# Eighteen chunks of neighbour rows fetched one row at a time instead of fifteen, with part of the issuing moved to ScalarE

## What is computed

```python
def gnn(x, edge_index, ...):
    src, dst = edge_index
    agg = segment_sum(x[src], dst, num_segments=6250)
    h = relu(agg @ W_rel + b_rel + x @ W_root)
    i, f, g, o = split(h @ W_ih.T + b_ih + b_hh, 4)
    c = sigmoid(i) * tanh(g)
    return (sigmoid(o) * tanh(c)) @ W_fc + b_fc
x = x + gnn(layernorm(x), stack([src, dst]), ...)
x = x + slice_attention(layernorm(x), ...)
```

## Time and profile before

| | us |
|---|---|
| Runs before | 1247.07, 1250.91, 1253.03 |
| Median | 1250.91 |
| The profiled execution | 1246.6 |
| Its span, first to last instruction | 1244.8 |
| Around the span | 1.8 |

### The profile page before, as it was taken

The page is one execution under the profiler, slowest core; times in us unless marked ns, Lnnn a source line. Parts: engine busy times, 40 slices in busy tenths (PEclk is TensorE's granted clock), DMA queues, the critical chain, the costliest instruction groups (busy, mean ns, idle before and its releaser), DMA issues. The chain is left out here.

```text
span 1244.8 us, 30252 instructions
## 1 busy us (share of the span) xinstructions
PE 1113.5 (89%) x9821; PEld 970.4 (78%) x9821; DVE 833.0 (67%) x2580; ACT 627.7 (50%) x1257; POOL 793.0 (64%) x836
## 2 busy tenths in 40 slices
PE   1056889999999999999999999999999999999998
PEld 0045778788888887888888877888888888897798
DVE  7885466677566856776667666766676667646665
ACT  6862435545454545544554455445645554545332
POOL 5367777777777777777777777777777777400000
PEclk9997899999999999999999999999999999999999
DMA  9574444544554445444544454444444554223498
GB/s 329 205 248 120 123 117 147 150 133 122 150 150 140 128 139 148 139 128 136 150 142 138 126 150 139 141 126 148 140 140 127 148 147 137 90 60 99 129 347 291
DMA packets 92942, 188.74 MB, mean 152 GB/s; under 512 B 20890, under 2 KB 55567, under 8 KB 92797
## 3 DMA queue, kind: packets, MB, share of 16 engines
q0 software_dynamic: 39168, 107.01, 30.4%
q1 hardware_dynamic: 42770, 59.89, 14.8%
q10 hardware_dynamic: 10859, 20.05, 4.5%
HBM read 154.87 MB, written 32.00 MB: 150 GB/s over the span
## 5 line engine op out<-in xcount | busy, mean ns | idle before, releaser
L676 POOL DMA_INDIRECT ring<-table,sidx x798 | 765.3, 959 | 266.0 <-issue 260.3
L414 PE MATMUL ps<-h_h,wih_h 128*128 128x250 f32 x1200 | 338.2, 282 | 0.0
L415 PE MATMUL ps<-h_l,wih_h 128*128 128x250 f32 x1200 | 336.0, 280 | 0.0
L416 PE MATMUL ps<-h_h,wih_l 128*128 128x250 f32 x1200 | 336.0, 280 | 0.0
L414 PEld LDWEIGHTS ps<-h_h,wih_h 128*128 128x128 f32 x1200 | 229.6, 191 | 2.0 <-issue 0.8
L415 PEld LDWEIGHTS ps<-h_l,wih_h 128*128 128x128 f32 x1200 | 229.6, 191 | 1.1
L416 PEld LDWEIGHTS ps<-h_h,wih_l 128*128 128x128 f32 x1200 | 229.5, 191 | 0.0
L820 ACT ACTIVATE gate<-ps,bgate 128x250 f32<-128x250 f32 x300 | 124.4, 468 | 138.3 <-PE ps L416 138.3
L1048 PE MATMUL ps<-ring,oneh 128*32 128x512 f16 x2280 | 147.3, 386 | 46.3 <-DMA ring<-table,sidx 35.5
L1475 DVE TENSOR_SCALAR oneh<-iota,didx 128x64 f16<-128x64 f16 (+2 forms) x1199 | 183.5, 259 | 0.9 <-issue 0.9
L1048 PEld LDWEIGHTS ps<-ring,oneh 128*32 128x32 f16 x2280 | 61.3, 97 | 114.4 <-DMA ring<-table,sidx 48.0
(11 more groups left out here) (212 smaller groups left out, 2499.2 us busy)
## 6 DMA issues: line engine op xcount, KB each, us to landing
sp_ring<-table SPq DMA_DIRECT2D x1920, 1.0 KB
ring<-table,sidx POOLq DMA_INDIRECT x798
swt_d<-swt ACTq DMA_DIRECT2D x25, 500.0 KB
gate<-swt_d SPq DMA_DIRECT2D x19, 500.0 KB, 5.7
x_room<-in_x SPq DMA_DIRECT2D x12, 512.0 KB, 10.5
xn<-table SPq DMA_DIRECT2D x25, 224.0 KB
xin<-in_x SPq DMA_DIRECT2D x25, 224.0 KB
res<-xin SPq DMA_DIRECT2D x25, 224.0 KB
```

The costliest lines, as they stand in the source:

```text
L414: eng.matmul(dst, wh, xh, start=first, stop=False)
L415: eng.matmul(dst, wh, xl, start=False, stop=False)
L416: return eng.matmul(dst, wl, xh, start=False, stop=last)
L676: pool.indirect_dma_start(ring[:, j, :], None, table, bass.IndirectOffsetOnAxis(ap=idx, axis=0)).then_inc(done, 16)
```

## The change

SP_STEP goes from 52 to 42 and SP_N from 15 to 18, so chunks 86, 128, ..., 800 leave POOL's list: three more than before. Of each such chunk SP fetches 104 rows, in register loads of 26, and ACT the other 24: 12 rows in turn 0, then 20 rows a turn in three places (6 after `split_x`, 8 after gates 0 to 3 and `tanh_c` 0, 6 after gates 8 and 9), with one register load of 24 words at the start of each chunk. SP's places and numbers of rows in a turn stay. `wait_slot`, the wait for a free slot of `sp_ring`, is now done by both engines. ACT's loop over turns is written out. PE's waits for `sp_ring` still count all 128 rows.

```diff
-    SP_FIRST, SP_STEP, SP_N, SP_SLOTS = 86, 52, 15, 3
+    SP_FIRST, SP_STEP, SP_N, SP_SLOTS = 86, 42, 18, 3
...
-    ROWS_FIRST, ROWS, LOADS = 96, (8, 16, 60), 32
+    ROWS_FIRST, ROWS, LOADS = 96, (8, 16, 60), 26
+    SP_ROWS = 4 * LOADS
+    ACT_ROWS = P - SP_ROWS
+    ACT_FIRST, ACT_PARTS = 12, (6, 8, 6)
...
+        def wait_slot(eng, k):
+            if k == 0:
+                eng.wait_ge(spi_done, 1)
+            if k >= SP_SLOTS:
+                b = last_reader(SP_CHUNKS[k - SP_SLOTS])
+                eng.wait_ge(sum_done[b % 2], b // 2 + 1)
+                eng.wait_ge(sum_done[(b - 1) % 2], (b - 1) // 2 + 1)
+
+        def load_starts(eng, starts, k, q, n):
+            _, at = nc.values_load_multi_w_load_instructions(
+                sp_idx[k:k + 1, q:q + n], engines=[eng.engine], min_val=0, max_val=(N - 1) * row_bytes,
+                skip_runtime_bounds_check_because="the DMA checks its bounds")
+            starts[:] = at
+
+        def fetch_row(eng, k, q, start):
+            to = sp_ring[q:q + 1, k % SP_SLOTS, :].bitcast(U8)
+            eng.dma_start(to, rows8[ds(start, row_bytes)].rearrange("(p c) -> p c", p=1)).then_inc(
+                sp_rows[k % SP_SLOTS], 16)
...
             def fetch_rows(n):
 
-                for r in range(row_at[0], min(row_at[0] + n, SP_N * P)):
-                    k, q = r // P, r % P
+                for r in range(row_at[0], min(row_at[0] + n, SP_N * SP_ROWS)):
+                    k, q = r // SP_ROWS, r % SP_ROWS
...
+            row_at, starts = [0], [0] * ACT_ROWS
+
+            def fetch_rows(n):
+
+                for r in range(row_at[0], min(row_at[0] + n, SP_N * ACT_ROWS)):
+                    k, q = r // ACT_ROWS, r % ACT_ROWS
+                    if q == 0:
+                        wait_slot(act, k)
+                        load_starts(act, starts, k, SP_ROWS, ACT_ROWS)
+                    fetch_row(act, k, SP_ROWS + q, starts[q])
+                row_at[0] += n
+
             def turn(t, odd, gather, gnn, ffn, ahead):
...
+                if t == 0:
+                    fetch_rows(ACT_FIRST)
                 if gnn:
                     split_x(t - 1)
+                    fetch_rows(ACT_PARTS[0])
                     relu_h(t - 1, 0)
...
                     gates(t - 1, 0, 4)
                     tanh_c(t - 1, 0)
+                    fetch_rows(ACT_PARTS[1])
...
                     gates(t - 1, 8, 10)
+                    fetch_rows(ACT_PARTS[2])
...
-            with act.Fori(lo, hi, step) as t:
+            for t in range(lo, hi, step):
                 two_turns(turn, t)
```

More of the change, by code:

```diff
@@ L429, in store_chunk @@
                 eng.dma_start(table[RP * P:N, :], lt[TILES][0:REST, 0, :]).then_inc(ln_out[k % TILES], 16)
+        rows8 = table.bitcast(U8).rearrange("n c -> (n c)")
+        row_bytes = 4 * C
+        def wait_slot(eng, k):
[14 more added lines that the diff above has]
+                sp_rows[k % SP_SLOTS], 16)
         @block.sync
@@ L508, in _ @@
             row_at = [0]
-            rows8 = table.bitcast(U8).rearrange("n c -> (n c)")
-            row_bytes = 4 * C
             def fetch_rows(n):
-                for r in range(row_at[0], min(row_at[0] + n, SP_N * P)):
-                    k, q = r // P, r % P
+                for r in range(row_at[0], min(row_at[0] + n, SP_N * SP_ROWS)):
+                    k, q = r // SP_ROWS, r % SP_ROWS
                     if q == 0:
[L517 to L522, removed]
-                    if q % LOADS == 0:
[L524 to L530, removed]
+                        wait_slot(sp, k)
+                    if q % LOADS == 0:
+                        load_starts(sp, starts, k, q, LOADS)
+                    fetch_row(sp, k, q, starts[q % LOADS])
                 row_at[0] += n
@@ L539, in turn @@
                     for j, k in SP_OF.items():
-                        assert first_reader(j) // 2 > t or row_at[0] >= (k + 1) * P, (t, j, k, row_at)
+                        assert first_reader(j) // 2 > t or row_at[0] >= (k + 1) * SP_ROWS, (t, j, k, row_at)
                 if gather:
@@ L570, in _ @@
             last_turns(turn)
-            assert row_at[0] >= SP_N * P
+            assert row_at[0] >= SP_N * SP_ROWS
             def f_load(n, k):
@@ L843, in copy_out @@
                                ACT.Copy).then_inc(att_a, 1)
-            def turn(t, odd, gather, gnn, ffn, ahead):
+            row_at, starts = [0], [0] * ACT_ROWS
[7 more added lines that the diff above has]
+                row_at[0] += n
+            def turn(t, odd, gather, gnn, ffn, ahead):
+                if gather and t < NP - 1:
+                    for j, k in SP_OF.items():
+                        assert first_reader(j) // 2 > t or row_at[0] >= (k + 1) * ACT_ROWS, (t, j, k, row_at)
+                if t == 0:
+                    fetch_rows(ACT_FIRST)
                 if gnn:
                     split_x(t - 1)
+                    fetch_rows(ACT_PARTS[0])
                     relu_h(t - 1, 0)
@@ L906, in _ @@
             lo, hi, step = turns(turn)
-            with act.Fori(lo, hi, step) as t:
+            for t in range(lo, hi, step):
                 two_turns(turn, t)
             last_turns(turn)
+            assert row_at[0] >= SP_N * ACT_ROWS
             def f_high(n, k):
```

## The result

| us | before | after |
|---|---|---|
| Median | 1251.97 | 1296.74 |
| Lowest to highest of four runs | 1247.07 to 1253.08 | 1293.56 to 1299.77 |
| The profiled execution | 1246.6 | 1299.77 |
| Its span | 1244.8 | 1298.0 |

The ratio is 1.0364 [1.0334, 1.0394]: slower by 3.6%. The forecast was 1247.2 with a range up to 1255, so it is wrong, in sign and in size. Lines have moved: L1048 is now L1081, L676 is L688, L524 is L446, L529 is L453, L546, L556 and L564 are L558, L568 and L576, L1063 is L1096, L1125 is L1158, L829 is L841, L1066 is L1099, L778 is L790.

The account below looks back on a forecast made before the run. POOL's gather stream up to block 48, plus a fixed 181.45 us of PE's work, was taken to set the end. -3.75 us from POOL and 0 from the rest gave 1250.91 - 3.75 = 1247.2 us, range 1241.5 to 1255.

Parts of the forecast that it names:

- SP: SP's queue: 84 rows a turn, loads of 26 words at 1.81 us, 5.9 us a turn after 5.6, all covered.
- The cover: SP's wait for the next transposes, 108.5 us over 22 turns, 4.9 each, was to hide 0.3 us more of loads.
- The gathers that go: POOL's list: three gathers less up to PE's last wait, at block 48, 3.75 us saved; bounds 0 to 7.5 us.
- ACT's rows: ACT's queue: 20 rows a turn at 0.318 us each, a 24-word load 1.71 us, nothing added to the total.
- Places 1 and 2: ACT after `split_x` and after L825: 3.6 and 4.25 us with a load, under 4.33 and 4.68 us idle; no cost.
- Place 3: ACT before L880: 1.9 us under 2.22; with a load 1.4 us late in four turns, 5.6 us, covered by PE's row waits.
- Waits for slots: SP and ACT waiting for a free slot of `sp_ring`, reused sooner with chunks every 42: costed at nothing.
- the one counted: Chunk 17, begun by SP in turn 21 and ACT in turn 20; its slot comes free in time, others have more room.
- The rivals: Dear ACT queue (0.12), no gain (0.14), more than three gathers (0.04), and a late chunk making PE wait for `sp_ring` (no separate chance).
- The one with the slower sign: ACT rows at 0.546 us, each waiting for SP's descriptor block; PE-bound, +16.6 us, 1267.5 us; chance 0.12.
- the rule of the Trainium skill that the prediction weighed: The descriptor-generating block is shared by two sequencers, locked by one at a time; at its strongest, the first rival's sum.
- my own signs for being wrong: PE's row waits vanish, L1125 waits longer every turn, SP waits in `wait_slot`, or POOL's period changes.

Follow-up runs that it names:

- kernel with one slow load: The changed kernel with SP's four register loads of a chunk at words 0, 26, 52 and 80: 1244.65 us, ratio 0.9976 to the kernel before.
- the 15-chunk experiment: The changed kernel with loads at words 0, 28, 52, 80 and the old 15 chunks, ACT still fetching 24 rows of each: 1246.91 us, ratio 0.9999.
- the first experiment: The changed kernel with SP's register loads at words 0, 28, 52 and 80 instead of 0, 26, 52 and 78: 1243.54 us, ratio 0.997.

## Why the prediction was wrong

**The step that failed is "SP": the price of a load of 26 words.** I took 1.81 us from a straight line between a load of one word and one of 32. Both of these begin at a multiple of four, and so do all the loads of the kernel before, so no row could show what the first word does. Measured: 2.1 us at words 0 and 52 (the line was nearly right there) and 5.6 us at words 26 and 78, so with the few longer ones 12.9 us of loads a turn instead of 5.9. My rows could have warned me in one way: I moved along the count of words alone, while the change also moved where the loads begin, and I gave that no upper bound. One word at 0.485 us was such a bound: 26 of them make 12.6 us.

The Trainium skill, "Runtime: NRT & Kernel Launch", section "Instruction fetch mechanics", says that a register load costs about 200 ns a register even in bulk; the page speaks of loads from HBM, and here the words lie in SBUF, the on-chip memory. The trace agrees off multiples of four (0.20 us a word) and not on them: 32 words took 2.13 us, where an estimate by the page's figure is 6.4 us.

**The cover was taken too large, and its consequence named nearly right.** I wrote that SP's 4.9 us of waiting a turn covers the loads, and that without it a load for the next block and then PE would be late. Of those 108.5 us, 33.5 stand behind SP's last row and cover nothing; while rows are left it is 3.8 us a turn. Either would have covered the 0.3 us that I forecast. The loads grew by 7.3 us a turn over the 5.6 of before, past the cover, and SP became the bound. The load that was late is that of x at L576, not that of the features at L558 before it in the queue. I did not go on to ask from which price of a load the cover is gone (some 2.9 us: 3.8 + 5.6 us over 84/26 loads), which would have made it a rival. The kernel with one slow load, at 2.93 us a load on average, bears that price out: it has no wait left and loses nothing. What no term of the prediction had is the 23 us by which SP may be behind before PE waits; it only puts the loss off.

**The gathers that go: right.** 3.75 us were forecast; with fast loads the change gives 3.5 us (1247.07 to 1243.54), and the chain's last wait for rows moved 3.0 us.

**ACT's rows: right in price and cover.** A row's DMA took 0.235 us in the median and rows follow each other every 0.32 us, as taken; a load of 24 words 1.74 us after 1.71. Places 1 and 2 cost nothing that shows: of all that ACT makes, PE's longer waits name only `sw`, which hangs on place 3. Place 3, in an ordinary turn and in one with a load, in the kernel with loads at multiples of four:

```profile
629.26 1.53 ACTq L454 DMA_DIRECT2D sp_ring<-table  x5
632.02 1.14 ACT L914 ACTIVATE sw_h<-ps 125x512 fp32r<-125x512 f32 x2 [2.33 <-DVE ps L1607]
...
670.70 3.64 ACTq L454 DMA_DIRECT2D sp_ring<-table  x5
674.44 1.09 ACT L914 ACTIVATE sw_h<-ps 125x512 fp32r<-125x512 f32 x2 [3.31 <-DVE ps L1607]
```

The rows end 1.2 us before `sw_h` could start, so there was more room than I took; with a load the copy's wait is 1.0 us longer (1.4 forecast). I expected the idle time shown before this copy to fall to 0.3 us; it did not, since the page does not count the issuing of DMAs as busy. PE's slack takes up the rest, as the 15-chunk experiment shows.

**Waits for slots: nearly right.** SP's waits in after name no earlier reader of a slot. With loads at multiples of four, where SP is not late, there is one, at 322 us, and the time does not show it:

```profile
SPq L447 <- PE ps L1083: 1.6, 1, 1.6
```

So it is not so that all chunks but the one counted have room to spare.

**The rivals.** None was the case. The one with the slower sign put the cost on ACT's queue and a shared descriptor block. The 15-chunk run at 0.9999 and the first experiment at 0.997, with all 20 rows a turn on ACT, rule that out for this kernel. So the rule of the Trainium skill that the prediction weighed ("Perfetto Trace Analysis", section "DMA Instruction — HWDGE (DVE, Sync)") costs this program nothing that shows. Of my own signs for being wrong, two came true: PE's waits for rows vanished, and POOL's period changed (gaps up to 7.6 us; the view names no releaser, and slots that a later PE frees later are the likely one).

## What to carry to other kernels

Cut batches of register loads where the first word is a multiple of four; two other places of four cost this kernel 4% (1.0364 against 0.997). A queue that only issues has a budget of one turn: add up its rows, transfers and register loads against its waits, and ask at which price of each the waits are gone, because below that nothing shows, and above it the queue falls behind until every turn pays. Leave out of the waits those that stand where the queue has nothing left to issue. And when a list is shortened, count it for every block that could be the last to wait, since the wait moves to the one that gained nothing.

## What was not expected

PE's stops cost it its clock. The granted clock (the last but two of the columns) around the longest stop, 8.7 us before 929.3:

```profile
912.00:920.60 8.60, 7.85 (x78) 5.14 (x76) 6.17 (x13) 5.75 (x12) 6.48 (x7) 1.00 0.57 172
920.60:929.30 8.70, 0.03 (x1) 0.00 (x1) 1.59 (x5) 0.00 (x0) 6.57 (x8) 0.74 0.62 196
...
931.00:933.00 2.00, 2.00 (x11) 2.00 (x11) 0.68 (x1) 1.67 (x5) 1.39 (x3) 0.50 0.26 70
933.00:935.00 2.00, 2.00 (x11) 2.00 (x10) 0.00 (x0) 0.00 (x0) 1.48 (x2) 0.50 0.45 133
935.00:940.00 5.00, 5.00 (x45) 5.00 (x44) 1.69 (x5) 1.37 (x3) 1.90 (x2) 1.00 0.27 81
```

It fell to 0.50, the level of 1.2 GHz, while PE stood still, stayed there up to 935 us with PE busy, and was at 2.4 GHz again after. PE's busy time rose by 15.0 us in all (1113.5 to 1128.5). In sums these are part of the 53.2 us of span. But SP's queue sets when the next x comes, and a faster PE would have waited longer for it, so they should not lengthen the span; that is argued from SP's gapless queue and was not tested by itself.

The other surprise is the register load itself: a factor of three between two loads of the same size, 1.6 and 5.1 us for 24 words, one word apart.
